# Transfers of the maxima issued ahead of the experts' weights, and twelve unread matmuls between the first scores

## The chip, the cores and the metric

The kernel runs on one core of a Trainium2 chip. A core has five engines that run side by side, each with its own instruction stream: TensorE (PE: matmuls and, as PEld, the loading of their stationary operand), VectorE (DVE), ScalarE (ACT), GpSimd (POOL) and SyncE (SP, which here only issues transfers). They meet through semaphores. Transfers between HBM and the core's memory, and inside that memory, run on 16 DMA engines. The metric is the device time of one execution in microseconds (us). TensorE's clock has two levels here, 2.4 and 1.2 GHz; the profile shows the granted one as PEclk, 1.00 for the higher.

## The reference

```python
def block(x, ctx, lens, Wg, W1, W3, W2, sw1, sw3, sw2):   # x, ctx: (8, 128, 256)
    # attention, 8 heads: the normed x asks, ctx is key and value, and the roles of
    # sequence (128) and width (256) are exchanged: 8 heads of 16 rows, 256 queries, 256 keys
    s = log(lens) / (8 * log(20))                          # one factor per batch entry
    q, k = layernorm(x) in heads of 16 rows, ctx in heads of 16 rows
    x = x + softmax(s * einsum('bhdq,bhdk->bhqk', q, k)) @ v
    # feed-forward: 8 experts of 352 hidden columns, top 1, 128 places each, and a shared one
    xt = layernorm(x).reshape(1024, 256)
    probs = softmax(xt @ Wg); e = argmax(probs); gate = probs[e]
    rows of xt go to their expert's first 128 free places, the rest is dropped
    oe = (silu(xd @ W1[e]) * (xd @ W3[e])) @ W2[e]
    shared = (silu(xt @ sw1) * (xt @ sw3)) @ sw2
    return x + oe[place] * gate * kept + shared
```

The text above is shortened from the reference; all tensors are float32.

## The kernel before

Everything is written out by hand for each engine, with semaphores between them. The first part is attention over 64 units n, one for each of 8 batch entries b and 8 heads. A head has 16 rows of the width-256 dimension, so each unit is a small matmul on 32 of the 128 rows of the array; four heads lie in four blocks of 32 rows.

Attention runs as a pipeline of turns t that every engine walks in the same order. In turn t:

- PE computes the scores of units 2t and 2t+1 (`scores`, L919; in the first LAG = 7 turns four units every second turn, L1030). Each unit is written in two halves u.
- DVE takes the negated row maxima of each unit (`maximum`, L500) into the tile `nm`.
- After the last unit of batch entry b, in turn 4b+4 (`MROW`, L108), PE transposes the maxima (`turn_maxima`, L928), ACT copies them to `mrow` (`maxima_rows`, L739), and SP transfers them from `mrow` into spare rows of the queries `qz` (`load_maxima`, L280 to L285), two transfers for each b. With the maximum as one more row of the contraction, the second scores come out already shifted.
- Seven turns behind, PE computes these shifted and transposed scores (`shifted_scores`, L940), ACT exponentiates them (L746), and PE weighs the values with them (`weigh_values`, L956, from turn 10 on).
- In turns 1 to 8 PE also transposes the context of each batch entry for the values (`turn_values`, L896; turn b+1), and ACT copies it (`values`, L725). Each transpose waits for the copy of the one before.
- `LATE` (L65) says in which turns DVE, ACT and POOL prepare the queries and keys of batch entries 2 and 3, 4 and 5, 6 and 7: statistics from turn 1, 7 and 14, scales and queries one turn later. On ACT, the copy of `values(1)` stands in turn 2 ahead of the statistics of entries 2 and 3 (L717, L719), and DVE's two operations that use them (L465, L468) stand between units 5 and 6 of `maximum`.

`shifted_scores` of the first unit of b waits for that entry's two transfers, `ld_m`. It is issued in turn 7 for b = 0, in turn 11 for b = 1, and so on.

Ahead of the pipeline PE runs 50 idle turns of four small matmuls on a tile of ones (`idle_turn`, L874).

SP issues its transfers strictly in this order: inputs x and context, the shared expert's weights (L319 to L326), then the weights of experts 1 to 4 (`load_expert`, L299 to L307, four transfers each), then a megabyte of zeros that clears the experts' rows in HBM (L330), then for each b the wait for `mrow` and its two transfers, then expert 0. Expert weights are first read after all shared up-projections are done (`expert_high`, L816). The second part of the kernel is the tokens' routing, the shared expert (`shared_up`, L1003 and L1005) and the experts; the change does not touch it.

X is PSUM bank 7, in which PE puts the transposed maxima, outputs and tokens.

Of the kernel before, what the change touches and what calls it, by code (L numbers as in the profile page):

```python
# [42 lines left out]
P = 128  # L43
# [4 lines left out]
E, C, F = 8, 128, 352  # L48
# [10 lines left out]
LAG = 7  # L59
FIRST = 12  # L60
IDLE_TURNS = 50
TURNS = NH // 2
CHUNKS = ((0, 1), (1, 2), (2, 4), (4, 6), (6, B))
EAGER = 2
# [14 lines left out]
NW = 5  # L79
DW = D + 2  # L80
NO_TOKEN = 4 * B * P
LOADS = ((0, 1), (1, 2), (2, 4), (4, E))

END = TURNS + LAG

# [52 lines left out]
def block_kernel(nc, x, ctx_in, lens, wg, w1, w3, w2, sw1, sw3, sw2, consts, out):  # L138
    with ExitStack() as es:
        def sb(name, shape, dt):  # L140
            return es.enter_context(nc.sbuf_tensor(name, shape, dt))

        def sem(name):
            return es.enter_context(nc.semaphore(name))


        xd_dram = nc.dram_tensor("expert_rows", [E * C, DW], F32, kind="Internal").ap()
# [5 lines left out]
        onesb = sb("onesb", [P, P], BF16)  # L153
# [53 lines left out]
        zero = sb("zero", [P, DW], F32)  # L207
# [17 lines left out]
        mx_bank, sc_bank, O, X = bank[0:NS], bank[NS:2 * NS], bank[6], bank[7]  # L225
# [10 lines left out]
        xd_zeroed, xd_sent = sem("xd_zeroed"), sem("xd_sent")  # L236
# [3 lines left out]
        empty_set, numbered = sem("empty_set"), sem("numbered")  # L240
# [32 lines left out]
        @block.sync  # L273
        def _(sp):
            def load_chunk(dst, src, i, done):

                a, z = CHUNKS[i]
                sp.dma_start(dst[:, a:z, :], src[a:z].rearrange("b p d -> p b d")).then_inc(done[i], 16)  # L278

            def load_maxima(b):  # L280

                sp.wait_ge(nm_row, b + 1)
                for half in range(2):
                    sp.dma_start(qz[HD * (1 - half):P:ROWS, b, half, :],
                                 mrow[4 * half:4 * half + 4, b % 2, :]).then_inc(ld_m[b % 2], 16)  # L285

            def load_expert(e):
                n = e % NW
                if e == 0:
                    sp.wait_ge(s_lo, len(SHARED_PIECES))  # L290

                if e == NW:
                    sp.wait_ge(e_up, 1)
                if e == NW + 1:
                    sp.wait_ge(ew_lo, 2)
                if e == NW + 2:
                    sp.wait_ge(ew_lo_2, 1)
                t = wts[n]
                sp.dma_start(t[:, W1:W3].rearrange("p (c f) -> p c f", c=DC),  # L299
                             w1[e].rearrange("(c p) f -> p c f", p=P)).then_inc(ld_w[n], 16)  # L300
                sp.dma_start(t[:, W3:W2].rearrange("p (c f) -> p c f", c=DC),
                             w3[e].rearrange("(c p) f -> p c f", p=P)).then_inc(ld_w[n], 16)
                if e >= NW:
                    sp.wait_ge(e_down, e - NW + 1)
                sp.dma_start(t[:, W2:W2 + 2 * D].rearrange("p (c d) -> p c d", c=2),  # L305
                             w2[e, 0:2 * P].rearrange("(c p) d -> p c d", p=P)).then_inc(ld_w[n], 16)
                sp.dma_start(t[0:FL, W2 + 2 * D:WCOLS], w2[e, 2 * P:F]).then_inc(ld_w[n], 16)  # L307

            load_chunk(xs, x, 0, ld_x)
            sp.dma_start(cst[:], consts).then_inc(ld_cst, 16)  # L310
            sp.dma_start(leni[:], bass.AP(tensor=lens.tensor, offset=lens.offset,
                                          ap=[[0, P], [1, B]])).then_inc(ld_len, 16)
            for i in range(1, len(CHUNKS)):
                load_chunk(xs, x, i, ld_x)
                if i >= EAGER:
                    load_chunk(cs, ctx_in, i, ld_ctx)

            s1 = sraw[:, S1:S3].rearrange("p (c f) -> p c f", c=DC)
            sp.dma_start(s1[:, :, 0:F], sw1.rearrange("(c p) f -> p c f", p=P)).then_inc(ld_shared, 16)  # L319
            sp.dma_start(s1[:, :, F:], wg.rearrange("(c p) f -> p c f", p=P)).then_inc(ld_shared, 16)  # L320
            sp.dma_start(sraw[:, S3:S2].rearrange("p (c f) -> p c f", c=DC),
                         sw3.rearrange("(c p) f -> p c f", p=P)).then_inc(ld_shared, 16)
            sp.dma_start(sraw[:, S2:S2 + 2 * D].rearrange("p (c d) -> p c d", c=2),
                         sw2[0:2 * P].rearrange("(c p) d -> p c d", p=P)).then_inc(ld_shared, 16)
            sp.wait_ge(pad_set, 1)
            sp.dma_start(sraw[0:FL, S2 + 2 * D:], sw2[2 * P:F]).then_inc(ld_shared, 16)  # L326
            for e in range(1, NW):
                load_expert(e)
            sp.wait_ge(empty_set, 2)
            sp.dma_start(xd_dram.rearrange("(n p) d -> p n d", p=P),  # L330
                         zero[:].unsqueeze(1).broadcast_to([P, E, DW])).then_inc(xd_zeroed, 16)
            for b in range(B):
                load_maxima(b)
            load_expert(0)

            sp.wait_ge(xd_sent, 16 * B)
            xd = xd_dram.rearrange("(n p) d -> p n d", p=P)
            for i, (a, z) in enumerate(LOADS):
                sp.dma_start(xe[:, a:z, :], xd[:, a:z, :]).then_inc(ld_xe[i], 16)

            for b in range(B):
                sp.wait_ge(shared_added, b + 1)
                sp.dma_start(out[b], xs[:, b, :]).then_inc(base_stored, 16)
            for e in range(NW, E):
                load_expert(e)
# [103 lines left out]
        def _(dve):  # L449
# [144 lines left out]
            for t in range(END + AFTER):  # L594
                if t < TURNS:
                    maximum(2 * t)
# [102 lines left out]
        def _(act):  # L699
# [82 lines left out]
            for t in range(END + AFTER):  # L782
# [6 lines left out]
                for when, work in ((OUT_COPY, copy_output), (TRSTD, token_rstd)):  # L789
                    if t in when:  # L790
                        work(when.index(t))
                if 0 <= t - LAG < TURNS:
                    exponentials(2 * (t - LAG))
# [75 lines left out]
        def _(pe):  # L869
# [7 lines left out]
            pe.wait_ge(ones_set, 1)  # L877
            for _ in range(IDLE_TURNS):
                for r in range(4):
# [25 lines left out]
            def scores(n, u):  # L905

                b, half, rows = place(n)
                scores_bank = bank[n % (2 * NS) if n < FIRST else n % NS]
                if n % H == 0 and u == 0:
                    if b < EAGER:  # L910
                        pe.wait_ge(k_eager, 2 * (b + 1))
                        pe.wait_ge(q_eager, b + 1)
                        pe.wait_ge(q_made, b + 1)
                    else:
                        pe.wait_ge(k_made, 2 * (b - EAGER + 1))
                        pe.wait_ge(q_made, 2 * (b + 1) - EAGER)
                if n >= 2 * NS and u == 0:
                    pe.wait_ge(maxed, n - 2 * NS + 1 if n < FIRST + NS else n - NS + 1)
                mm = nc.tensor.matmul(scores_bank[:, u * D:(u + 1) * D], qz[rows, b, half, u * P:(u + 1) * P],  # L919
                                      kz[rows, b, half, :], start=True, stop=True)  # L920
                if u == 1:
                    mm.then_inc(scored, 1)
# [102 lines left out]
            for t in range(END + AFTER):  # L1025
                for m in range(NG):
                    for c in range(2):
                        if t == WEIGH[m][c]:
                            weigh_values(m, c)
                if t < LAG and t % 2 == 0:  # L1030
                    heads = range(2 * t, min(2 * t + 4, 2 * LAG))
                    for u in range(2):
                        for n in heads:
                            scores(n, u)
                for part in range(2):
                    for k in range(2):
                        if LAG <= t < TURNS:
                            scores(2 * t + k, part)
                        if 0 <= t - LAG < TURNS:
                            shifted_scores(2 * (t - LAG) + k, part)  # L1040
                for b in range(B):
                    if t == VALUES[b]:
                        turn_values(b)
                for when, work in ((MROW, turn_maxima), (OUT_TURN, turn_output), (OUT_BACK, turn_back),
                                     (TTURN, turn_tokens)):
                    if t in when:
                        work(when.index(t))

                if t in EARLY_UPS:
                    shared_up(EARLY_UPS[t])  # L1050
                if t == EARLY_COUNT:
                    count_tokens(0)
# [136 lines left out]
```

## Time and profile before

| | |
|---|---|
| median of 3 runs | 194.24 us (193.72 to 194.97) |
| the profiled execution | 194.63 us, span 192.7 us |
| mean granted clock | 0.886 |
| PE / PEld busy | 159.4 us (83%) / 112.5 us (58%) |
| DVE, ACT, POOL busy | 104.7, 84.6, 62.7 us |
| DMA queue of SP and ACT | 14240 packets, 14.98 MB |

The span runs from the first to the last instruction. Windows are given in us from its start. The busy time of PE is that of the matmuls in flight, so a PE at 100% may still do little if its matmuls are on few rows or at the lower clock. A wait is put down to the semaphore that came last.

### The profile page before, as it was taken

Reading aid. Unit: us, or ns where it says so; the run is one execution under the profiler, and the core shown is the slowest. Engines: PE = TensorE matmul, PEld = TensorE weight load, DVE = VectorE, ACT = ScalarE, POOL = GpSimd, SP = SyncE. Lnnn points to the kernel's source line nnn. Section 1 sums busy time; section 2 is a strip of 40 time slices with the busy share of each in tenths; the row PEclk is TensorE's granted clock in tenths of the full one; section 3 lists DMA queues with packets and bytes.
Section 4 is the critical chain, followed back from the end, with each engine's and each line's share of the span. In section 5 each row is a group of like instructions: output and inputs, shape, how many; then the busy total and the mean of one; then the engine's idle time right before and its main releaser. Section 6 shows DMA issues by size and latency. Waiting matters only on the chain.

```text
span 192.7 us, 3827 instructions
## 1 busy us (share of the span) xinstructions
PE 159.4 (83%) x1448; PEld 112.5 (58%) x1448; DVE 104.7 (54%) x241; ACT 84.6 (44%) x189; POOL 62.7 (33%) x85
## 2 busy tenths in 40 slices
PE   7679505999998999999999687299893999979960
PEld 7445103555545455555455387298792889779840
DVE  1497202525795978777341433423868238598530
ACT  2632000544747585665757363514751155465000
POOL 5158000092027081432202000044085058535241
PEclk9975555557999999999999999969999799999996
DMA  4999990000000000000070000002025845983001
GB/s 131 343 342 329 322 333 24 0 5 2 2 5 2 3 2 3 2 3 2 0 228 1 2 0 0 3 31 82 0 82 153 292 123 154 306 269 140 29 22 54
DMA packets 15697, 18.44 MB, mean 96 GB/s; under 512 B 1852, under 2 KB 14949, under 8 KB 15680
## 3 DMA queue, kind: packets, MB, share of 16 engines
q1 hardware_dynamic: 14240, 14.98, 25.1%
q0 software_dynamic: 1152, 2.97, 4.6%
q10 hardware_dynamic: 288, 0.26, 0.4%
q8 instruction: 11, 0.18, 0.4%
q14 instruction: 6, 0.05, 0.1%
HBM read 14.12 MB, written 4.21 MB: 95 GB/s over the span
## 4 chain that ended last, share of the span: by engine, by line
PE 62%; SPq 11%; DVE 10%; issue 4%; DMA 4%; POOL 3%; ACT 2%; another core or an unknown queue 2%; DVEq 0%; POOLq 0%; ACTq 0%
PE bank L919 12%; PE bank L940 9%; PE bank L956 8%; PE bank L1003 5%; PE bank L1005 4%; PE bank L1150 4%; DMA qz<-mrow 4%; PE bank L1080 3%; PE bank L1124 3%; PE bank L1125 3%; SPq L278 3%; PE bank L968 2%; SPq L305 2%; DVE xlo L639 2%
## 5 line engine op out<-in xcount | busy, mean ns | idle before, releaser
L500 DVE TENSOR_REDUCE nm<-bank 128x2 f32<-128x512 f32 x64 | 41.1, 685 | 27.4 <-PE bank L919 27.3
L940 PE MATMUL bank<-qz,kz 32*128 32x256 f32 x256 | 46.5, 443 | 9.2 <-DMA qz<-mrow 9.2
L919 PE MATMUL bank<-kz,qz 32*128 32x256 f32 x256 | 43.9, 472 | 2.1 <-POOL qz L358 1.5
L746 ACT ACTIVATE pt<-bank 128x512 f32<-128x512 f32 x64 | 34.6, 589 | 18.0 <-PE bank L940 17.9
L940 PEld LDWEIGHTS bank<-qz,kz 32*128 32x128 f32 x256 | 27.9, 204 | 15.7 <-issue 11.2
L919 PEld LDWEIGHTS bank<-kz,qz 32*128 32x128 f32 x256 | 25.8, 217 | 15.8 <-DVE nm L500 7.4
L956 PE MATMUL bank<-pt,vext 128*32 128x256 f32 x256 | 21.1, 406 | 0.0
L358 POOL TENSOR_SCALAR qz<-xs,rs,mrs 128x256 f32<-128x256 f32 x14 | 7.7, 565 | 39.4 <-DVE mrs L468 39.4
L420 POOL DMA_INDIRECT expert_rows<-rk,idx_s x8 | 8.1, 1012 | 32.6 <-DVE rk L586 30.8
L1150 PE MATMUL bank<-wraw,kz 128*128 128x256 f32 (+1 forms) x48 | 11.8, 386 | 1.8 <-DVE hTlo L646 1.4
L725 ACT COPY vext<-bank 128x256 f32<-128x256 f32 x8 | 3.0, 370 | 23.2 <-PE bank L896 23.2
L443 POOL DMA_INDIRECT out<-vext,rk x8 | 8.2, 1027 | 13.6 <-DVE vext L665 7.2
L436 POOL DMA_INDIRECT vext<-out,rk x8 | 9.2, 1154 | 10.4 <-DMA out<-xs 8.2
L1080 PE MATMUL bank<-shi,hThi 128*128 128x256 f32 x24 | 8.2, 341 | 4.4 <-DVE hTlo L625 4.3
L1150 PEld LDWEIGHTS bank<-wraw,kz 128*128 128x128 f32 (+1 forms) x48 | 8.7, 190 | 3.6 <-DVE kz L660 2.0
L383 POOL TENSOR_TENSOR mrs<-mv,rstd 128x1 f32<-128x1 f32 x6 | 1.1, 189 | 28.3 <-ACT rstd L758 28.3
L956 PEld LDWEIGHTS bank<-pt,vext 128*32 128x32 f32 x256 | 5.2, 110 | 7.2 <-issue 6.2
L591 DVE TENSOR_TENSOR qz<-bank,cs 128x352 f32<-128x352 f32 x8 | 4.1, 522 | 9.3 <-ACT cs L775 7.9
L536 DVE TENSOR_TENSOR xlo<-bank,xhi 128x256 fp32r<-128x256 f32 x8 | 3.4, 425 | 10.5 <-ACT xhi L762 10.5
L639 DVE TENSOR_TENSOR xlo<-wraw,xhi 128x704 fp32r<-128x704 f32 x8 | 8.6, 1112 | 0.0
L1003 PE MATMUL bank<-shi,xhi 128*128 128x360 f32 x16 | 5.9, 367 | 3.3 <-issue 2.8
L1080 PEld LDWEIGHTS bank<-shi,hThi 128*128 128x128 f32 x24 | 5.3, 220 | 5.5 <-DVE hTlo L625 5.3
(140 smaller groups left out, 316.7 us busy)
## 6 DMA issues: line engine op xcount, KB each, us to landing
wraw<-in_w SPq DMA_DIRECT2D x16, 352.0 KB, 7.5
wraw<-in_w SPq DMA_DIRECT2D x8, 256.0 KB, 7.5
expert_rows<-zero SPq DMA_DIRECT2D x1, 1032.0 KB, 10.3
out<-xs SPq DMA_DIRECT2D x8, 128.0 KB, 3.5
xs<-in_x SPq DMA_DIRECT2D x3, 256.0 KB, 6.1
cs<-in_ctx SPq DMA_DIRECT2D x3, 256.0 KB, 6.3
wraw<-in_w SPq DMA_DIRECT2D x8, 96.0 KB, 8.1
wraw<-in_sw SPq DMA_DIRECT2D x2, 352.0 KB, 4.5
```

Source lines behind the costliest of these rows:

```text
L420: nc.gpsimd.indirect_dma_start(xd_dram, bass.IndirectOffsetOnAxis(ap=idx_s[:, b:b + 1], axis=0), x2[:, b, :], None, bounds_check=E * C - 1 ...
L436: nc.gpsimd.indirect_dma_start(res[:, e, :], None, out_rows, number(e), bounds_check=B * P - 1, oob_is_err=False).then_inc(gathered[e], 16)
L443: nc.gpsimd.indirect_dma_start(out_rows, number(e), res[:, e, :], None, bounds_check=B * P - 1, oob_is_err=False).then_inc(out_sent, 16)
L500: nc.vector.tensor_reduce(nm[:, b % 2, :, place], scores_bank[:].rearrange("p (u c) -> p u c", u=2), AX_X, ALU.max, negate=True).then_inc( ...
L639: nc.vector.tensor_tensor(elo[e % 2][:, a:z], wts[e % NW][:, a:z], ehi[e % 2][:, a:z].bitcast(F32), ALU.subtract).then_inc(ew_lo, 1)
L746: nc.scalar.activation(pt[:, g % NPT, n % 4, :], sc_bank[n % NS][:], ACT.Exp).then_inc(exped, 1)
L919: mm = nc.tensor.matmul(scores_bank[:, u * D:(u + 1) * D], qz[rows, b, half, u * P:(u + 1) * P], kz[rows, b, half, :], start=True, stop=True)
L940: mm = nc.tensor.matmul(sc_bank[n % NS][:, c * D:(c + 1) * D], kz[rows, b, half, c * P:(c + 1) * P], qz[rows, b, half, :], start=True, sto ...
L956: mm = nc.tensor.matmul(O[32 * j:32 * j + 32, g * D:(g + 1) * D], vext[:, b, c, h, :], pt[:, m % NPT, i, c * D:(c + 1) * D], start=(c == 0 ...
L1003: nc.tensor.matmul(u1, xpart[:, b, c, :], weights(part, S1, F + WG, c, F + WG), start=a, stop=z)
L1080: mm = nc.tensor.matmul(y_bank[b % 2][:, 0:D], hpart[:, b % 2, c * P:(c + 1) * P], weights(part, S2, D, c, D), start=(k == 0), stop=(k == ...
L1150: mm = nc.tensor.matmul(y_bank[(e + 1) % 2][:, 0:D], hTe[0:rows, e % 2, c * P:(c + 1) * P], wts[e % NW][0:rows, W2 + c * D:W2 + (c + 1) * ...
```

## The change

Two edits. SP's list is rewoven: the wait and the two transfers of the maxima of b now stand ahead of the weights of expert b+1, for b = 0 to 3, and the zeros stand behind the maxima of b = 4. PE runs six matmuls of 512 columns over the tile of ones into bank X behind the scores of turn 0 and six behind those of turn 2; nothing reads their result.

```diff
+UNREAD = {0: 6, 2: 6}
...
-            for e in range(1, NW):
-                load_expert(e)
-            sp.wait_ge(empty_set, 2)
-            sp.dma_start(xd_dram.rearrange("(n p) d -> p n d", p=P),
-                         zero[:].unsqueeze(1).broadcast_to([P, E, DW])).then_inc(xd_zeroed, 16)
             for b in range(B):
                 load_maxima(b)
+                if b + 1 < NW:
+                    load_expert(b + 1)
+                if b + 1 == NW:
+                    sp.wait_ge(empty_set, 2)
+                    sp.dma_start(xd_dram.rearrange("(n p) d -> p n d", p=P),
+                                 zero[:].unsqueeze(1).broadcast_to([P, E, DW])).then_inc(xd_zeroed, 16)
             load_expert(0)
...
                     for u in range(2):
                         for n in heads:
                             scores(n, u)
+                    for _ in range(UNREAD.get(t, 0)):
+                        nc.tensor.matmul(X[:].rearrange("p (n c) -> p n c", c=P), onesb[:],
+                                         onesb[:].unsqueeze(1).broadcast_to([P, 4, P]), start=True, stop=True)
```

On SP, this is the end of the initial loads in the kernel before: the weights of the fourth expert (`wraw<-in_w`), the zeros (`expert_rows<-zero`), all sixteen transfers of maxima (`qz<-mrow`), and the first transfer of expert 0.

```order
L299 DMA wraw<-in_w 128x2x352
L301 DMA wraw<-in_w 128x2x352
L305 DMA wraw<-in_w 128x2x256
L307 DMA wraw<-in_w 96x256
L330 DMA expert_rows<-zero 128x8x258
L284 DMA qz<-mrow 4x256 x16
L299 DMA wraw<-in_w 128x2x352
```

In the changed kernel, SP goes on like this behind the last transfer of the shared weights (its line numbers are one higher).

```order
L327 DMA wraw<-in_sw 96x256
L285 DMA qz<-mrow 4x256 x2
L300 DMA wraw<-in_w 128x2x352
L302 DMA wraw<-in_w 128x2x352
L306 DMA wraw<-in_w 128x2x256
L308 DMA wraw<-in_w 96x256
L285 DMA qz<-mrow 4x256 x2
L300 DMA wraw<-in_w 128x2x352
```

The first two transfers of maxima have moved from behind sixteen transfers of weights and the zeros to the place ahead of them.

On PE, turns 0 to 7 before: scores (`bank<-kz,qz`), transposes for the values (`bank<-cst,cs`), the transpose of the first maxima (`bank<-cst,nm`), and the first shifted scores (`bank<-qz,kz`).

```order
L919 MATMUL bank<-kz,qz 128x256 x8
L896 MATMUL bank<-cst,cs 128x128 x2
L919 MATMUL bank<-kz,qz 128x256 x8
L896 MATMUL bank<-cst,cs 128x128 x4
L919 MATMUL bank<-kz,qz 128x256 x8
L896 MATMUL bank<-cst,cs 128x128 x2
L928 MATMUL bank<-cst,nm 8x128 x2
L896 MATMUL bank<-cst,cs 128x128 x2
L919 MATMUL bank<-kz,qz 128x256 x4
L896 MATMUL bank<-cst,cs 128x128 x2
L919 MATMUL bank<-kz,qz 128x256
L940 MATMUL bank<-qz,kz 128x256
```

The same stretch of the changed kernel, up to the transpose of the maxima (line numbers two higher).

```order
L921 MATMUL bank<-kz,qz 128x256 x8
L1038 MATMUL bank<-onesb 128x512 x6
L898 MATMUL bank<-cst,cs 128x128 x2
L921 MATMUL bank<-kz,qz 128x256 x8
L1038 MATMUL bank<-onesb 128x512 x6
L898 MATMUL bank<-cst,cs 128x128 x4
L921 MATMUL bank<-kz,qz 128x256 x8
L898 MATMUL bank<-cst,cs 128x128 x2
L930 MATMUL bank<-cst,nm 8x128 x2
```

The two groups of six stand between the scores and the transposes for the values; nothing else on PE changed its place.

## Rows read from the trace of the kernel before

**Rows 1.** The page's strip of transfers: the span in 40 slices of 4.8 us.

```profile
GB/s 131 343 342 329 322 333 24 0 5 2 2 5 2 3 2 3 2 3 2 0 228 1 2 0 0 3 31 82 0 82 153 292 123 154 306 269 140 29 22 54
```

**Rows 2.** Waits from 7 to 32 us: who for whom, us, times, longest.

```profile
PE bank L940 <- DMA qz<-mrow: 9.2, 1, 9.2
```

**Rows 3.** Chain of work that ended last, 17 to 36 us: start, us, what.

```profile
23.89 7.01 DMA qz<-mrow
...
31.04 0.76 PE bank L940
```

**Rows 4.** Instructions in order of time: start, us, engine (q: its sequencer), line.

```profile
17.26 0.36 ACT L739 COPY mrow<-bank 8x256 f32<-8x256 f32 x1
...
21.40 3.00 SPq L284 DMA_DIRECT2D qz<-mrow  x2
```

**Rows 5.** The same view, 7 to 21 us, PE, DVE and ACT.

```profile
7.51 1.15 PE L919 MATMUL bank<-kz,qz 32*128 32x256 f32 x16 [1.52 <-POOL qz L358]
...
9.53 2.48 DVE L500 TENSOR_REDUCE nm<-bank 128x2 f32<-128x512 f32 x4
...
11.92 0.57 PE L896 MATMUL bank<-cst,cs 128*128 128x128 f32 x2
...
12.53 0.37 ACT L725 COPY vext<-bank 128x256 f32<-128x256 f32 x1 [2.53 <-PE bank L896]
...
13.63 2.54 PE L919 MATMUL bank<-kz,qz 32*128 32x256 f32 x16
...
14.23 1.28 DVE L500 TENSOR_REDUCE nm<-bank 128x2 f32<-128x512 f32 x2
...
16.59 0.63 PE L928 MATMUL bank<-cst,nm 128*8 128x128 f32 x2
...
20.57 1.22 PE L919 MATMUL bank<-kz,qz 32*128 32x256 f32 x2
```

**Rows 6.** Windows: length, busy PE PEld DVE ACT POOL, clock, DMA share, GB/s.

```profile
12.00:13.00 1.00, 0.49 (x2) 0.12 (x2) 1.00 (x6) 0.46 (x2) 0.09 (x1) 0.54 1.11 320
```

**Rows 7.** Windows by stage, same columns.

```profile
15.60:20.60 5.00, 4.87 (x22) 2.33 (x17) 3.04 (x5) 1.11 (x3) 3.12 (x6) 0.50 1.08 319
20.60:31.00 10.40, 1.19 (x3) 0.46 (x2) 0.74 (x2) 0.37 (x1) 0.00 (x0) 0.50 0.90 275
31.00:46.55 15.55, 15.52 (x100) 8.35 (x100) 6.46 (x14) 5.62 (x13) 5.71 (x10) 0.51 0.01 2
46.55:50.42 3.87, 3.87 (x54) 2.12 (x51) 2.58 (x4) 2.88 (x6) 0.00 (x0) 1.00 0.01 2
68.63:77.47 8.84, 8.84 (x108) 4.82 (x107) 7.01 (x14) 5.57 (x14) 4.23 (x7) 1.00 0.01 3
97.80:101.20 3.40, 3.40 (x34) 1.84 (x34) 1.56 (x5) 2.02 (x4) 0.00 (x0) 1.00 0.88 295
101.20:104.60 3.40, 3.40 (x34) 1.72 (x32) 0.15 (x1) 3.12 (x8) 1.41 (x2) 1.00 0.02 2
```

**Rows 8.** Instructions in order of time, where turn 12 begins.

```profile
46.55 0.64 PE L956 MATMUL bank<-pt,vext 128*32 128x256 f32 x8
```

**Rows 9.** The maxima of b = 2: the copy, then a window of half a microsecond.

```profile
49.30 0.34 ACT L739 COPY mrow<-bank 8x256 f32<-8x256 f32 x1
...
51.30:51.80 0.50, 0.50 (x14) 0.48 (x11) 0.50 (x1) 0.33 (x1) 0.00 (x0) 1.00 0.03 8
```

**Rows 10.** Instructions in order of time: idle turns, and 118 to 119 us.

```profile
1.01 4.97 PE L874 MATMUL bank<-onesb 32*128 32x128 bf16 x200 [1.01 <-POOL onesb L352]
...
118.84 0.33 PE L1003 MATMUL bank<-shi,xlo 128*128 128x360 f32 x1
119.00 0.32 PE L1005 MATMUL bank<-shi,xlo 128*128 128x352 f32 x1
```

**Rows 11.** Instructions in order of time, PE alone, 121 to 125 us.

```profile
121.03 0.44 PE L983 MATMUL bank<-cst,rk 128*128 128x128 f32 x2 [1.70 <-DVE rk L531]
...
124.38 0.40 PE L1003 MATMUL bank<-shi,xhi 128*128 128x360 f32 x1 [2.83 <-issue]
```

## The prediction

> **What bounds the kernel now.** I read the stages first, then the waits, then the chain. The page's strip of transfers shows the queue full from 5 to 29 us [rows 1]. Over the same time the table by stage shows PE doing little: from 20.6 to 31.0 us it is busy for 1.19 of 10.40 us [rows 7]. The waits name one event: `shifted_scores` of turn 7 waits 9.2 us for the transfer of the first maxima [rows 2]. The chain says the same: 7.01 us of `qz<-mrow`, then L940 at 31.04 [rows 3]. The maxima themselves were ready long before: ACT wrote them by 17.62, SP issued them only at 21.40 [rows 4], because sixteen transfers of weights and the zeros stand ahead, and the 8 KB then had to go through a queue that those had filled. Nothing else ends that wait.
>
> The second thing is the clock. It is at the lower level, 1.2 GHz, from 12.5 us [rows 6] until just before 46.55, where PE's window reads 0.51 and the next one 1.00 [rows 7]. Before it fell, PE ran only scores 4 to 7, sixteen instructions on 32 rows each like the group at 7.51 [rows 5], and a transpose, and waited for DVE between them. In the lower state turns 7 to 11 took 15.5 us (31.04 to 46.55) [rows 3, 8], 3.1 us each; turns 12 and 13 then took 3.87 us, 1.94 each, and a block of four turns with every kind of work in it 8.84, 2.21 each [rows 7]. PE sets the pace in both. In all windows shown behind turn 12, up to 104.6 us, PE is busy throughout [rows 7], so whatever turn 12 gains should arrive at the end.
>
> **The change part by part.** I follow PE to two moments: the start of turn 7 (31.04 before) and of turn 12 (46.55 before).
>
> *The unread matmuls.* Their price has no row. The nearest from below is the shared up-projection, two instructions of 360 columns 0.16 us apart [rows 10]: 512 columns would be 0.23, six 1.4 us. From above, the idle turns: four blocks of 128 columns side by side per 0.0994 us (4.97/50) [rows 10] make 512 columns 0.40, six 2.4 us. At the higher clock I take 1.4, since the up-projection also uses all 128 rows and stands at that level.
>
> The first six start at 8.66 and end about 10.1. DVE takes its first maximum only at 9.53 and is busy with four until 12.01 [rows 5], and scores 4 to 7 need only be there by then, so these six are hidden; if DVE were not late they would cost their 1.4 us. The second six start where `turn_values(1)` stood, 11.92, and are not hidden: that transpose, and ACT's copy behind it at 12.53 [rows 5], come 1.4 us later. Behind this copy ACT holds the statistics of entries 2 and 3; DVE's scales wait for them and stand ahead of units 6 and 7 of the maxima (14.23 to 15.51) [rows 5]. Before, the scales had about no slack, so units 6 and 7 end about 1.2 us later, at 16.7. On PE, scores 8 to 11 took 2.54 us from 13.63 at the lower clock; at the higher the like-sized group took 1.15 [rows 5]. They start at about 15.0 and end at 16.1, before DVE's 16.7. So the transpose of the maxima comes at 16.8 instead of 16.59, and ACT's copy ends at about 17.7 instead of 17.62. The two effects nearly cancel.
>
> *The transfers of the maxima.* SP now issues at 17.7. What it has issued by then is x, the context, the constants and the shared weights, 3.35 MB by their shapes, which at 343 GB/s [rows 1] is 9.8 us: the queue is empty at about 13. For an empty queue, the maxima of b = 2: copied by 49.64, last bytes moved between 51.3 and 51.8 [rows 9], so 1.7 to 2.2 us. The bound from above is what happened before, 9.5 us from issue to landing (21.40 to 30.9), which the full queue made. I take 2.2: landing at 19.9. PE is there by about 18.5 (before 20.57 [rows 5], with 5 us of work from 15.6 at the lower clock [rows 7]), so it waits some 1.4 us and turn 7 starts at 19.9. Gain there: 31.04 - 19.9 = 11.1 us.
>
> *Turns 7 to 11.* If the clock is held, they go at 1.94 to 2.21 us a turn [rows 7], 9.7 to 11.1 us. DVE alone bounds them from below: two maxima 1.28 us [rows 5] in every turn and one us of statistics, at least 7.4. Turns 7 to 9 have no weighing yet, 7 and 8 have a transpose for the values more. I take 2.0, 10.0 us: turn 12 at 29.9 instead of 46.55. Gain there: 16.6 us, of which 5.5 come from the clock in these turns.
>
> *The weights and zeros.* They now run during attention, 5.3 MB or 16 us of the queue at 343 GB/s, each of the four experts between two groups of maxima. From 97.8 to 101.2 us such weights ran at 295 GB/s and PE began 34 instructions, as many as in the 3.4 us behind it at 2 GB/s [rows 7]; so I price their company at nothing. They land by about turn 20 and are first read after 110 us; were that cover gone, an expert's 1056 KB would cost 3.6 us at 295 GB/s. SP has nothing else queued behind its new waits until expert 0, whose place is the same.
>
> *Sum.* 194.63 (the profiled execution) - 16.6 = 178.0. Its time is 0.4 above the median shown, so 177.6 for the median.
>
> **Whether the clock stays up** is what I know least. Between the second six (end 13.3) and turn 7 (19.9) PE has scores 8 to 13 and a row of transposes, and waits at the end. One row for such a stretch: around 121 us PE had two transposes and little else between 119.2 and 124.4, with waits of 1.70 and 2.83 us [rows 11], and behind it the clock was at the lower level for a while. My stretch is denser, and the one that preceded the fall at 12.5 had the waits without the unread matmuls. I lean to the clock being held. The Trainium skill ("TensorE: Matmul & The Clock Gate", Part 4: PE-mode transpose) says that work in transpose mode does not count for the gate as matmuls do. If so, PE's transposes between the two groups and turn 7 do not help, and the clock falls there, as in the first rival below: by that rule 183.1 where the sum says 177.6. The row at 121 us agrees with it as far as it goes, but waits stand beside the transposes there, so it doesn't separate them.
>
> **The rivals.**
> - *The clock falls while PE transposes and waits for the maxima* (about 16 to 20 us). Turn 7 starts at 19.9, but turns 7 to 11 take their 15.5 us as before: turn 12 at 35.4, gain 11.1, 183.1 for the median. For it: those turns at the lower clock did not bring it back until their end, although PE was busy for 15.52 of 15.55 us [rows 7]. A fall only after two or three of these turns gives about 180.
> - *The unread matmuls don't hold the clock at 12.5 us.* The second six then cost up to 2.4 us, DVE and PE are late by 1.5 to 2, turn 7 starts at about 22.5: gain 8.5, 185.7. Against it: full rows for 2.8 us in a stretch where PE was on quarter rows.
> - *The wait stays, behind other weights.* Maxima of b = 1 to 4 now follow an expert each. If a group lands only behind the expert ahead of it, with 3.6 us of transfer and up to 9.5 us from issue, against three turns of slack (5.8 us), four waits of 3.7 us make 15 us. With the clock lost too (gain 11.1) the kernel would be slower, at 198; with the clock held, 192.4. It decides only if an expert's weights are still in the queue when the next copy is done; but SP issues them 8.8 us (four turns) earlier, against 3.6 us of transfer. Little speaks for it.
> - *The first wait was not the queue*: the transfers take 9.5 us even on an empty queue. Then turn 7 starts at 27.2, and a PE that waits so long again keeps no clock: gain 3.8, 190.4. The copy of b = 2 [rows 9] speaks against it.
>
> **How the numbers follow.** Clock held 0.52; falls before or in the first turns of turn 7 and later 0.30; not held at 12.5 us 0.12; wait stays behind other weights 0.03, of which 0.02 end slower; first wait not the queue 0.03. The case of 177.6 has its own range of 175.5 (turns 7 to 11 near DVE's bound) to 179.5 (2.21 a turn, and stretches of low clock that shift in the last part). For 8 in 10 the range must take in the falling clock, 180 to 184, so 175.5 to 185.0. About 1% is what a measurement of this kernel can tell from no change. All cases of a shorter first wait are faster by more: 0.96 faster, 0.02 same, 0.02 slower.
>
> **What would show it.** Right: no wait of L942 longer than 2 us; `qz<-mrow` issued at 17 to 18 us and nothing of `wraw<-in_w` ahead of it; clock 1.00 from 9 to 50 us; turn 12 (first L958 of the third group) at about 30 us; transfers low after 13 us, and the experts' weights in bursts of 3 to 4 us until about 60. Wrong: clock 0.50 at 22 us (first rival) or at 13 (second); a wait of L942 on `qz<-mrow` in turns 11, 15 or 19 (third). If turn 12 comes at 30 and the end is not 16 us earlier, the gain was given back behind attention, which I hold to be unchanged.

## The result and the profile after

| | before | changed |
|---|---|---|
| median of 4 runs | 193.98 us (192.56 to 194.97) | 178.21 us (176.30 to 181.00) |
| ratio of the faster executions | | 0.911 (95% interval 0.901 to 0.921) |
| profiled execution / its span | 194.63 / 192.7 | 181.00 / 178.1 |
| first scores (L919, L921) | 7.51 | 8.47 |
| transpose of the first maxima (L928, L930) | 16.59 | 18.05 |
| turn 7: first shifted scores (L940, L942) | 31.04 | 21.32 |
| turn 12: its weighing (L956, L958) | 46.55 | 31.25 |
| last group of weighing starts | 107.41 | 91.98 |

By the medians the change is faster by 15.8 us, 8.1%, and 0.6 us from the 177.6 forecast. The ratio of 0.911 counts only two of the changed kernel's four executions, those of 176.30 and 176.86 us, which ran at a mean granted clock of 0.974 and 0.971; the other two took 179.55 us (0.950) and, the profiled one, 181.00 us (0.955). The same kernel run again (e0 below) gave 0.921. The times in the table are from the profiled executions; rows of the changed kernel have line numbers two higher on PE, DVE and ACT, and one higher on SP.

Where the 9.2 us wait was, the chain of the changed kernel (start, length, what) goes straight through:

```profile
8.47 2.02 PE bank L921 x16
10.49 2.16 PE bank L1038 x6
12.66 0.22 PE bank L898 x2
12.88 1.07 PE bank L921 x16
13.95 1.40 PE bank L1038 x6
15.35 0.23 PE bank L898 x2
...
15.61 0.37 ACT vext L727
15.98 0.20 ACT lnv L719
...
16.21 0.21 ACT rstd L721
...
16.44 0.17 DVE rs L467
...
16.80 1.21 DVE nm L502 x2
...
18.05 0.40 PE bank L930 x2
...
18.48 0.37 ACT mrow L741
...
18.86 0.66 SPq L285
...
19.57 1.61 DMA qz<-mrow
...
21.32 0.45 PE bank L942
```

Both groups of unread matmuls (L1038) stand on it, then ACT's copy and the statistics behind it, DVE's scales and its next two maxima, and the maxima's own path. The transfer takes 1.61 us on the chain instead of 7.01 [rows 3]. The same steps in order of time show PE's wait for it, 0.32 us where there were 9.2 [rows 2], and DVE's for ACT:

```profile
16.44 0.16 DVE L467 SCALAR_TENSOR_TENSOR rs<-rstd,lnown 128x4 f32<-128x4 f32 x1 [1.18 <-ACT rstd L721]
...
18.86 1.21 SPq L285 DMA_DIRECT2D qz<-mrow  x2
...
21.32 0.45 PE L942 MATMUL bank<-qz,kz 32*128 32x256 f32 x1 [0.32 <-DMA qz<-mrow]
```

By stage, with the columns of [rows 7] (length, busy PE PEld DVE ACT POOL, clock, DMA share, GB/s):

```profile
9.00:11.00 2.00, 2.00 (x18) 1.05 (x11) 1.34 (x5) 0.97 (x2) 1.52 (x3) 0.50 1.09 359
11.00:13.00 2.00, 2.00 (x12) 0.88 (x13) 2.00 (x5) 0.09 (x1) 1.33 (x3) 0.75 0.98 317
13.00:21.00 8.00, 7.27 (x60) 3.91 (x57) 6.61 (x16) 2.91 (x9) 4.10 (x8) 1.00 0.04 12
21.32:31.25 9.93, 9.15 (x100) 5.33 (x100) 6.78 (x16) 5.63 (x14) 4.64 (x9) 1.00 0.49 151
31.25:92.00 60.75, 59.43 (x671) 32.01 (x670) 40.07 (x86) 38.84 (x89) 18.84 (x28) 1.00 0.26 85
...
105.00:116.00 11.00, 7.57 (x34) 7.50 (x35) 3.82 (x16) 3.40 (x8) 3.23 (x4) 0.69 0.07 26
```

Turns 7 to 11 take 9.93 us with a hundred PE instructions at clock 1.00, where the same hundred took 15.55 at 0.51 [rows 7]. In windows of 0.2 us the clock fell at 8.6 us and was back at 12.0 (hence 0.75 in the row from 11 to 13); after that it was low only for a while in the last part. The fall came before the first unread matmul, which starts at 10.4. The experts' weights run beside the turns (151 GB/s) instead of ahead of them.

### The profile page after: what moved, and what is told of

The parts are those of the page before. It is cut to its first block, busy times and chain, and to the rows that moved or that the text cites. A ratio compares the mean times of both kernels' runs of the same rounds, so it can differ in the third digit from the quotient of the medians.

```text
span 178.1 us, 3851 instructions
## 1 busy us (share of the span) xinstructions
PE 152.3 (85%) x1460; PEld 109.1 (61%) x1460; DVE 105.7 (59%) x241; ACT 84.8 (48%) x189; POOL 63.8 (36%) x85
## 4 chain that ended last, share of the span: by engine, by line
PE 66%; DVE 12%; DMA 7%; issue 4%; ACT 4%; POOL 3%; SPq 1%; POOLq 0%; ACTq 0%; DVEq 0%
PE bank L921 12%; PE bank L958 8%; PE bank L942 8%; PE bank L1005 5%; PE bank L1007 5%; PE bank L1155 5%; PE bank L1085 4%; PE bank L1129 3%; PE bank L1130 3%; DMA wraw<-in_w 3%; DVE xlo L641 3%; DMA leni<-in_lens 3%; PE bank L970 2%; DVE nm L502 2%; PE bank L1038 2%
## 5 line engine op out<-in xcount | busy, mean ns | idle before, releaser
L942 PE MATMUL bank<-qz,kz 32*128 32x256 f32 x256 | 41.2, 403 | 1.1 <-ACT pt L748 0.8
L921 PE MATMUL bank<-kz,qz 32*128 32x256 f32 x256 | 36.3, 420 | 2.5 <-POOL qz L360 2.5
L921 PEld LDWEIGHTS bank<-kz,qz 32*128 32x128 f32 x256 | 21.7, 190 | 13.3 <-issue 8.9
L942 PEld LDWEIGHTS bank<-qz,kz 32*128 32x128 f32 x256 | 24.9, 184 | 6.7 <-ACT pt L748 4.2
L958 PE MATMUL bank<-pt,vext 128*32 128x256 f32 x256 | 20.2, 391 | 0.0
L445 POOL DMA_INDIRECT out<-vext,rk x8 | 9.0, 1123 | 12.8 <-DMA vext<-out,rk 6.1
L641 DVE TENSOR_TENSOR xlo<-wraw,xhi 128x704 fp32r<-128x704 f32 x8 | 10.0, 1283 | 0.0
L958 PEld LDWEIGHTS bank<-pt,vext 128*32 128x32 f32 x256 | 5.2, 108 | 6.6 <-issue 6.3
L777 ACT ACTIVATE cs<-bank 128x352 f32<-128x352 f32 x8 | 3.6, 464 | 11.1 <-PE bank L1007 11.0
```

Of the source, the lines that this page charges most:

```text
L445: nc.gpsimd.indirect_dma_start(out_rows, number(e), res[:, e, :], None, bounds_check=B * P - 1, oob_is_err=False).then_inc(out_sent, 16)
L641: nc.vector.tensor_tensor(elo[e % 2][:, a:z], wts[e % NW][:, a:z], ehi[e % 2][:, a:z].bitcast(F32), ALU.subtract).then_inc(ew_lo, 1)
L942: mm = nc.tensor.matmul(sc_bank[n % NS][:, c * D:(c + 1) * D], kz[rows, b, half, c * P:(c + 1) * P], qz[rows, b, half, :], start=True, sto ...
L958: mm = nc.tensor.matmul(O[32 * j:32 * j + 32, g * D:(g + 1) * D], vext[:, b, c, h, :], pt[:, m % NPT, i, c * D:(c + 1) * D], start=(c == 0 ...
```

## Experiments

Every kernel was run with a profile and then, unless said otherwise, three more times, beside the kernel before on the same chip. The kernel before gave medians of 194.50 us beside e0 to e3, 193.31 beside e5 to e8 and 193.82 beside e9 to e12. Leaving one execution of the kernel before of 449 us aside, it stayed between 192.4 and 195.2 throughout.

| run | median, range (us) | turn 7 | first scores to L930 | mean clock of the executions |
|---|---|---|---|---|
| changed, first profile | 178.21 (176.3 to 181.0) | 21.32 | 9.58 | 0.955 0.950 0.974 0.971 |
| e0 changed again | 178.52 (177.7 to 179.6) | 20.83 | 9.59 | 0.950 0.954 0.961 0.956 |
| e1 maxima only | 182.70 (178.8 to 184.5) | 21.19 | 9.35 | 0.912 0.912 0.909 0.949 |
| e2 unread only | 194.13 (191.9 to 196.1) | 30.80 | 9.59 | 0.895 to 0.914 |
| e3 transposes | 177.00 (175.9 to 177.6) | 18.35 | 7.33 | 0.968 0.967 0.966 0.968 |
| e5 second six only | 178.04 (176.9 to 183.9) | 21.23 | 10.14 | 0.906 0.967 0.965 0.960 0.957 |
| e6 twenty-four | 181.17 (178.2 to 182.7) | 21.33 | 10.53 | 0.974 0.926 0.937 0.952 |
| e7 75 idle turns | 177.80 (177.3 to 178.5) | 20.70 | 7.91 | 0.967 0.968 0.964 0.965 |
| e8 75, no unread | 178.24 (176.1 to 184.2) | 21.25 | 8.11 | 0.949 0.974 0.913 0.961 |
| e9 behind the values | 178.45 (176.9 to 185.3) | 18.93 | 7.33 | 0.961 0.946 0.964 0.916 |
| e10 transposes, behind | 178.41 (176.2 to 181.9) | 18.54 | 7.78 | 0.970 0.966 0.934 0.936 |
| e11 weights last | 179.68 (177.0 to 180.2) | 20.18 | 9.59 | 0.956 0.957 0.954 0.964 |
| e12 transposes again | 177.81 (175.5 to 178.3) | 19.95 | 8.38 | 0.955 0.965 0.962 0.967 |

Turn 7 and the distance are of the profiled execution, the first of each list of clocks. Of the other executions only the time and the mean clock are known: that one "lost the clock" is read from a mean of 0.90 to 0.94 together with a long time, and where in the kernel it was lost is not shown. The first scores themselves start between 7.3 and 8.5 us with 50 idle turns, whatever the kernel (9.5 and 9.9 with 75); what moves them is told in the last section.

### The two parts apart (e0, e1, e2)

e0 is the changed kernel. 

> The changed kernel as it is, beside the runs below on the same chip. Theory (wait gone and clock held): turn 7 at 20 to 21.5 us, clock 1.00 from there to past 100 us, 176 to 180 us. Rival (part of the executions lose the clock in the first turns): the times of single executions fall in two groups, some near 177 and some at 180 or above.

178.52 us, 0.921 (0.914 to 0.929) of before. Turn 7 at 20.83; the clock was low from 8.2 to 11.6 us, then at 1.00 to past 100. No execution reached 180 us, as the rival had it. There are two at 177.7 and 177.8 and two at 179.2 and 179.6, but their mean clocks (0.961 and 0.950, 0.956 and 0.954) do not set these pairs apart.

e1 leaves the unread matmuls out.

```diff
-UNREAD = {0: 6, 2: 6}
+UNREAD = {}
```

> Only the transfers of the maxima are moved; no unread matmuls. If the two parts are worth what the prediction says (11.1 us the wait, 5.5 us the clock), this is about 183 us: turn 7 (first L942) at 20 to 21 us, the clock at 0.50 there, and turns 7 to 11 take about 15.5 us. Rival, the clock is held by the missing wait alone: about 178 us, and the unread matmuls are worth nothing.

182.70 us. The profiled execution is the forecast's first rival in pure form (same columns):

```profile
9.00:13.00 4.00, 3.10 (x22) 1.61 (x20) 3.55 (x10) 1.59 (x5) 2.85 (x5) 1.00 1.00 314
13.00:21.00 8.00, 7.34 (x34) 4.34 (x34) 5.92 (x14) 2.35 (x7) 4.30 (x8) 0.54 0.08 17
21.00:34.00 13.00, 13.00 (x80) 7.20 (x78) 6.03 (x14) 4.91 (x12) 4.83 (x10) 0.50 0.38 125
34.00:50.00 16.00, 14.92 (x188) 8.12 (x188) 12.75 (x27) 10.75 (x24) 4.88 (x8) 1.00 0.33 104
```

The clock fell at 13.6 us and was back at 34.0, and PE walked turns 7 to 10 at 0.50 with its matmuls in flight for 13.00 of 13.00 us. Turn 7 came at 21.19, as with the unread matmuls, turn 12 at 36.07 instead of 30.77. But one of the four executions had a mean clock of 0.949 and took 178.79 us, as the changed kernel does. So without unread work the clock is lost often, not always. The parts are then 11.3 to 11.8 us for the transfers (to 193.98 and 194.50), and 4.2 us by the medians for the unread matmuls. These 4.2 us are a matter of how often the clock is kept: three of four executions lost it here, none of eight of the changed kernel; an execution that keeps it is no slower without them.

e2 keeps the unread matmuls and has SP's order as before.

> Only the twelve unread matmuls; SP's order as before. Theory: the wait for the first maxima stays until about 31 us, PE stands idle for 10 us, the clock falls in it whatever was run before, turns 7 to 11 take 15.5 us: 194 us, within 1% of before. Rival, the unread matmuls help by themselves: below 191.5 us with the clock at 1.00 before 40 us.

194.13 us in ten executions, ratio 0.998 (0.993 to 1.003). The stages:

```profile
12.60:22.60 10.00, 7.52 (x62) 4.11 (x60) 7.21 (x16) 3.00 (x9) 4.32 (x9) 0.99 1.09 321
22.80:30.80 8.00, 0.00 (x0) 0.03 (x1) 0.00 (x0) 0.00 (x0) 0.00 (x0) 0.50 0.94 282
30.80:46.50 15.70, 15.70 (x104) 8.37 (x108) 6.45 (x14) 5.62 (x13) 5.71 (x10) 0.51 0.01 3
```

and its wait:

```profile
PE bank L941 <- DMA qz<-mrow: 10.0, 1, 10.0
```

Here too the clock was low from 8.7 to 12.1 us. Then, with the unread matmuls on PE, it stayed at 1.00 where the kernel before ran at 0.50; PE stood still for the maxima from 21 us, the clock fell at 22.3, and turns 7 to 11 took what they had before. Alone, this part is worth nothing: its 4.2 us exist only once the wait is gone.

### What kind of unread work (e3, e12)

```diff
-nc.tensor.matmul(X[:].rearrange("p (n c) -> p n c", c=P), onesb[:],
-                 onesb[:].unsqueeze(1).broadcast_to([P, 4, P]), start=True, stop=True)
+nc.tensor.transpose(X[:, 0:P], cs[:, 0, 0:P], ident)
```

> As the changed kernel, but the twelve unread matmuls of 512 columns are twelve unread fp32 transposes of 128 columns, which the profile of before shows at the same 0.21 us each. If a transpose keeps the clock as a matmul does: 176 to 180 us, clock 1.00 in turns 7 to 11. If transposes do not count for the clock as matmuls do: turn 7 at the same time, but the clock at 0.50 in turns 7 to 11, about 183 us, as with no unread work at all.

177.00 us, 0.910 (0.904 to 0.917), the four executions within 1% of each other. The clock stayed at 1.00 from 7 us to past 100:

```profile
7.00:13.00 6.00, 4.77 (x48) 3.48 (x48) 5.33 (x17) 2.72 (x8) 3.40 (x6) 1.00 1.00 315
13.00:18.00 5.00, 4.72 (x36) 2.79 (x36) 4.96 (x11) 2.17 (x7) 4.07 (x8) 1.00 0.08 25
18.35:28.29 9.94, 9.16 (x100) 5.33 (x100) 6.79 (x16) 5.63 (x14) 4.64 (x9) 1.00 0.51 155
28.30:89.00 60.70, 59.38 (x668) 31.98 (x666) 40.09 (x86) 38.83 (x89) 18.76 (x28) 1.00 0.26 84
```

So the transposes, as this kernel issues them, did the unread matmuls' work. They are also shorter than I had expected of them:

```profile
8.83 0.88 PE L1038 MATMUL bank<-cst,cs 128*128 128x128 f32 x6
9.54 0.38 PE L898 MATMUL bank<-cst,cs 128*128 128x128 f32 x2
9.86 1.65 PE L921 MATMUL bank<-kz,qz 32*128 32x256 f32 x16
11.43 0.87 PE L1038 MATMUL bank<-cst,cs 128*128 128x128 f32 x6
```

Six end in 0.88 us instead of the matmuls' 1.47. Turn 7 started at 18.35, 2.5 us before e0: 0.2 by earlier first scores, the rest by a distance of 7.33 instead of 9.59, most of it because the clock never fell (with the matmuls and no fall, e7 below, it is 7.91).

e12 is the same kernel on another chip. 

> The kernel with unread transposes at the places of the twelve matmuls once more, beside the two above on the same chip. Theory: 176 to 178 us and, as the first time, all executions within 1%; the changed kernel's executions spread over 1 to 2.5%. Rival, the first time was luck of the clock: executions above 180 us among them.

177.81 us, 0.909 (0.902 to 0.917). Here the clock did fall in the profiled execution, from 9.5 to 12.9 us, and turn 7 came at 19.95. None of the eight executions of e3 and e12 took more than 178.3 us or had a mean clock below 0.955; the eight of the changed kernel lie between 176.3 and 181.0. The medians of the eights are 177.4 and 178.5; the intervals of the ratios overlap, so "0.6% better" is not shown. No run found a version that is clearly better than the change.

### Which group, and how much (e5, e6)

e5 keeps the second group alone.

```diff
-UNREAD = {0: 6, 2: 6}
+UNREAD = {2: 6}
```

> As the changed kernel, with the six unread matmuls behind turn 2 only. The first six cost 2.2 us where they ran at the lower clock. Theory: the clock in turns 7 to 11 hangs on the stretch from 12 to 20 us, which the second six fill, so it is held without the first, and turn 7 starts 1 to 2 us earlier: 176 to 178 us. Rival, the first six are needed to bring the clock back after it fell at about 9 us: clock 0.50 in turns 7 to 11 of the profile, 181 to 184 us.

178.04 us. The profiled execution took 183.87 and is the only one of five that lost the clock in the turns:

```profile
8.00:14.80 6.80, 6.80 (x39) 3.98 (x40) 5.31 (x14) 1.68 (x5) 2.85 (x5) 0.53 0.77 242
15.00:21.00 6.00, 5.20 (x40) 2.77 (x38) 4.60 (x10) 2.62 (x8) 4.18 (x8) 1.00 0.00 1
21.70:35.00 13.30, 13.30 (x88) 6.66 (x83) 6.08 (x14) 5.40 (x13) 5.71 (x10) 0.50 0.46 157
```

The clock was low from 7.6 us, came back at 14.4 while the second six ran (13.27 to 15.1), and fell again at 21.2. The other four took 176.9 to 180.0, as the changed kernel. With one in five against none in eight, the worth of the first six stays open.

e6 has twelve in each place.

```diff
-UNREAD = {0: 6, 2: 6}
+UNREAD = {0: 12, 2: 12}
```

> Twenty-four unread matmuls, twelve behind turn 0 and twelve behind turn 2. It prices them. If only the second group lies on the path, as predicted (1.4 us for six), 1.4 us more than the changed kernel: 180 us. If both groups do, 2.8 us or more: 181 to 182 us. If neither does, no change: 178.5 us.

181.17 us, in the range of the case in which both groups lie on the path. But the median doesn't price the matmuls: the two longest executions, 182.4 and 182.7 us, ran at a mean clock of 0.926 and 0.937, and the profiled one, at 0.974, took 178.22 us. The profile does. It has no fall of the clock before 100 us, and DVE's wait for ACT in the place named above:

```profile
16.46 0.16 DVE L467 SCALAR_TENSOR_TENSOR rs<-rstd,lnown 128x4 f32<-128x4 f32 x1 [2.48 <-ACT rstd L721]
```

From the first scores to the transpose of the maxima it takes 10.53 us, against 7.91 in e7, the kernel with twelve whose clock did not fall: 2.6 for twelve more matmuls, 0.22 each. So beyond twelve, every unread matmul in either place stands on the path in full.

### More work ahead of the scores (e7, e8)

```diff
-IDLE_TURNS = 50
+IDLE_TURNS = 75
```

> The changed kernel with 75 idle turns ahead of the scores instead of 50, so that PE is not idle from 6 to 8 us. In the changed kernel the clock fell at about 9 us for 3.4 us, with the first six unread matmuls in it. Theory: that fall comes from PE's idle time between the idle turns and the first scores; with it filled the clock is 1.00 from 6 us on, the first six take 1.4 instead of 2.2 us, turn 7 starts 1 to 2 us earlier: 176 to 177 us, and single executions lie closer together. Rival, the fall has another cause: same as the changed kernel, 178.5 us.

177.80 us, 0.918 (0.910 to 0.926). The clock did not fall before 100 us, the first six took 1.47, and the four executions lie within 0.7%, as the theory had it. But turn 7 came hardly earlier (20.70 against 20.83 in e0), since the first scores came later:

```profile
8.43 1.27 PE L876 MATMUL bank<-onesb 32*128 32x128 bf16 x77 [2.64 <-issue]
9.51 0.47 PE L921 MATMUL bank<-kz,qz 32*128 32x256 f32 x4
```

In the middle of the idle turns PE stood for 2.64 us, waiting for nothing that the profile shows. So the gap was moved, not filled, and the theory, that the fall comes from it, was not tested by this run. Other profiles speak against it: in e9 PE stood for 3.11 us ahead of the first scores and the clock did not fall, in e11 for 1.86 and it did. The queries were ready at 8.14 us here, and PE came to the scores only at 9.51.

e8 takes the unread matmuls out of this kernel.

> 75 idle turns, the maxima first, and no unread matmuls. Theory: it is PE's thin work from 9 to 20 us that loses the clock; more work before it does not help: clock 0.50 in turns 7 to 11, 182 to 184 us, like the kernel with the maxima only. Rival, the idle turns do the unread matmuls' work at no price on the path: 175 to 177 us.

178.24 us: neither theory. In the profile the clock fell at 8.5 us and came back at 12.0 with no unread work behind the scores (77 of the idle matmuls ran from 8.17 to 10.15), and stayed at 1.00 through turns 7 to 11; of the other three executions one, at 0.913 and 184.2 us, lost it. So it behaves as e1 does, one in four here against three in four there; that the idle turns made this difference is not shown by four executions each.

### The place on PE (e9, e10)

In both, the unread work of turns 0 and 2 stands behind `turn_values(0)` and `turn_values(1)` instead of ahead of them: e9 with the matmuls, e10 with the transposes of e3.

```diff
+for _ in range(UNREAD.get(t, 0)):     # now behind turn_values(b) of turn t; UNREAD = {1: 6, 2: 6}
```

> The changed kernel with the second six unread matmuls behind the transpose of values(1) instead of ahead of it (the first six behind that of values(0), in the same gap). In the changed kernel the step that made them cost was: transpose, ACT's copy, the statistics of entries 2 and 3 behind it on ACT, DVE's scales, and only then maxima 6 and 7. Theory: with the transpose ahead of them they fill the time in which PE waits for ACT's copy anyway; DVE's scales come right behind its maxima 4 and 5, and turn 7 starts 1 us earlier: about 177 us against 178.5. Rival, the place does not matter: 178.5 us.

In the profiled execution the step is as the theory says. ACT's copy comes at once, and DVE's scales follow its own maxima without a wait:

```profile
12.64 0.37 ACT L727 COPY vext<-bank 128x256 f32<-128x256 f32 x1 [2.37 <-PE bank L898]
...
12.90 1.26 DVE L502 TENSOR_REDUCE nm<-bank 128x2 f32<-128x512 f32 x2
13.02 0.29 ACT L719 ACTIVATE lnv<-mv,epst 128x2 f32<-128x2 f32 x1
...
14.07 0.15 DVE L467 SCALAR_TENSOR_TENSOR rs<-rstd,lnown 128x4 f32<-128x4 f32 x1
```

The distance to L930 is 7.33 us, as in e3, instead of 7.91 with the clock up in both (e7), and 9.59 in e0. So at the higher clock the place is worth 0.6 us. Yet the median is 178.45, no better: one execution lost the clock and took 185.3, one took 179.6.

> Twelve unread transposes in place of the twelve matmuls (0.145 us each in the run with transposes, against 0.23), behind the transposes of the values as in the run before. Theory: the shortest unread work at the place where it costs least, so the earliest turn 7, at 18 to 18.5 us, and 175.5 to 176.5 us. Rival, with so little work so late the clock falls in some executions: 176 to 182 us with a wide spread.

178.41 us, 0.909 (0.903 to 0.915) by the two executions of 176.2 and 176.5 us. Turn 7 at 18.54 was as expected, but the other two ran at 0.934 and 0.936 and took 180 to 182. That is what the rival said of the times; where these two lost the clock was not profiled.

### The company of the weights (e11)

SP's list has the weights of experts 1 to 4 and the zeros behind the maxima of b = 7.

> The changed kernel with the weights of experts 1 to 4 and the zeros behind all maxima, so that no large transfer runs during attention until about 80 us. It prices the company of these transfers and their place between the maxima. Theory (they cost nothing): turns 12 to 36 take the same time to 0.3 us, turn 7 starts at the same time, and the end is the same unless the weights are now late for the experts: 178 to 179 us. Rival, the transfers slow PE, ACT or DVE or delay maxima: turns 12 to 36 are shorter by 1 us or more.

179.68 us, 0.918 (0.910 to 0.926). From the weighing of turn 12 to the last group of weighing, in e11 and then in e0:

```profile
30.12 0.64 PE L957 MATMUL bank<-pt,vext 128*32 128x256 f32 x8
...
90.84 1.07 PE L957 MATMUL bank<-pt,vext 128*32 128x256 f32 x16
```

```profile
30.77 0.64 PE L958 MATMUL bank<-pt,vext 128*32 128x256 f32 x8
...
91.49 1.07 PE L958 MATMUL bank<-pt,vext 128*32 128x256 f32 x16
```

60.72 us in both, and from the first scores to turn 7 12.84 and 12.85. The weights between the maxima cost attention nothing that these two profiles show, neither by their traffic nor by their place in the queue. The median is 0.7 us above the forecast's range. In the profile the part behind the last weighing takes 85.8 us against 84.5 in e0; the weights now come there (260 GB/s from 90.8 to 103 us), but that they cause the 1.3 us was not tested.

## Why the prediction was right, and where it was not

**The wait for the maxima** was the queue, as forecast. From the transpose of the maxima to turn 7 I had 3.1 us (16.8 to 19.9); it took 3.27, and 3.25 to 3.26 in e0, e3 and e9. With a queue emptied of weights the transfer takes 1.61 us on the chain. The rival in which it takes 9.5 us on an empty queue is gone. Turn 7 came 9.7 us earlier, not 11.1: 1.0 of the difference is the later start of the scores (8.47 against 7.51), which follows the landing of `in_lens` and not the change (last section), 0.3 the distance to the transpose of the maxima (the price of the unread matmuls, below), 0.2 the path behind it.

**Turns 7 to 11** I had at 10.0 us at the higher clock; they took 9.93, and 9.94 in e0 and e3. With it the gain at turn 12 is 15.3 us instead of 16.6, and it reached the last weighing unchanged: from turn 12 to there 60.73 us against 60.86 before. Behind it 86.1 us against 85.3; the clock was low there for longer (0.69 over eleven us, against 0.84 over the like eleven before, from 120.4 us). That is why the profiled execution gained 14.6 us in its span.

**The sum.** It was made for the profiled execution: 194.63 - 16.6 = 178.0. That execution took 181.00, so the sum missed by 3.0: 1.3 at turn 12, 0.7 from there to the end of the span, and 1.0 outside the span (1.9 before, 2.9 after), for which the prediction had no term. That the median comes to 0.6 us of the forecast is in part luck: it is the middle of two executions near 176.6 and two near 180.3, and none of the four took 177 to 179. The four of e0 lie closer to it, with a median of 178.52.

**The price of the unread matmuls.** 0.23 us each at the higher clock: six took 1.40 on the chain, as forecast; 2.16 at the lower. The failed step is "these six are hidden", said of the first group. They were costed against DVE, which indeed waited only 0.17 us for scores 4 to 7. But `turn_values(1)` stands behind both groups, and through ACT's copy it sets DVE's scales; I had counted that chain for the second group alone. The chain above carries both, and e6 prices both. A second slip went the other way: "about no slack" for DVE's scales. In the kernel before, ACT's statistics ended at 13.44 and the scales started at 13.96, 0.5 us of slack; and the scores and transposes around the unread work, at the higher clock, get there sooner. So where the clock never falls the twelve together lengthen the distance by about 0.6 us (7.91 in e7, 7.33 in e9 and e3), not by the 1.2 that I had for the second six alone. In the profiled execution the low clock from 8.6 to 12.0 us ate that: distance 9.58 us, beside the 9.3 that I had in effect. That these two numbers are close is luck.

**The clock.** "Clock 1.00 from 9 to 50 us" was wrong in the profile: it was low from 8.6 to 12.0 us. The prediction also read the fall before at 12.5 us; its own row (0.54 from 12 to 13) puts it at 12.1. In the changed kernel the clock came back at 12.0 while the first six ran (10.43 to 12.66); in e5, which has scores there instead, it stayed low with PE in flight for 6.80 of 6.80 us and came back at 14.4, while its only six ran. From this pair it looks as if dense unread work brings the clock back early, but that is argued: e8 was back at 12.0 without any. That unread work keeps the level in turns 7 to 11 rests on none of eight executions that lost it with the matmuls, none of eight with the transposes of e3 and e12, and three of four without. The level in turns 7 to 11, which mattered for the sum, was as forecast.

**The first rival** (clock lost in the turns, 183.1 us) is what e1 is in three of four executions (182.3 to 184.5), and what single executions of e5, e8 and e9 are (183.9 to 185.3; those of e8 and e9 by time and mean clock alone). None of the eight of the changed kernel has a mean clock below 0.950. The page's rule that spoke for it (the Trainium skill, "TensorE: Matmul & The Clock Gate", Part 4: PE-mode transpose) is not borne out by the transposes of this kernel: in e3 they were all the unread work there was, and the clock was 1.00 from 7 us on. Whether they run in the mode that the page means, no row shows. The measurement decides.

**The second rival**, clock not held at 12.5 us: in the profile it fell earlier, at 8.6, for 3.4 us, and was back when the second six ran, so they cost 1.40 and not 2.4. **The third**, a wait behind other weights: of all 256 matmuls of L942 only the first waits for `qz<-mrow`, for 0.3 us, and e11 gives the same 60.72 us.

What stays open is why an execution keeps the clock and the next, with the same kernel, does not. e1, e5, e6, e8, e9 and e10 show that it happens, with no unread work and with up to twenty-four matmuls of it; four executions of each are too few to rank them.

## What to carry to other kernels

A small transfer that a compute engine waits for belongs ahead of bulk loads that are needed later, if the issuing engine can afford the wait for its data; look for it as one long wait on a transfer whose source was written long before. Ahead of a stretch in which TensorE sets the pace, thin work and a standstill can cost twice, once in time and once in the clock of what follows (turns 7 to 11: 15.5 us at 0.51, 9.9 at 1.00); unread work there paid only after the standstill itself was gone. Count what stands behind such filler on its own engine through every chain, and judge it by several executions, since the clock of one proves little.

## What was not expected of the hardware

- Six unread fp32 transposes of 128 columns took 0.88 us, although a pair of the same kind is shown at 0.38. The time of a group holds the tail of its last matmul: by these two groups four more cost 0.50, 0.13 each. In the same way six more matmuls of 512 columns cost 1.29 (2.76 for twelve in e6, 1.47 for six), 0.22 each.
- PE stopped for 2.64 us (e7) and 1.92 us (e8) inside 300 independent matmuls on one tile, both times behind the 223rd, with no wait that the profile shows. What it waits for there was not tested. In e7 the queries were ready at 8.14 us and in e8 at 7.00, and the scores came at 9.51 and 9.88, so more filler ahead of the scores delayed them.
- The start of the first scores moved by 1.1 us (7.34 to 8.47) between executions of kernels with the same instructions up to there. With 50 idle turns it follows one small transfer, `in_lens`: DVE converts the lengths as soon as they land, and the scales and the first queries wait for that. The conversion (L481, `lenf<-leni`, waiting for the transfer of `leni`) started at 5.30 us in the kernel before, 5.13 in e11, 5.77 in e0 and 6.26 in the changed kernel, and the first scores came 2.21 us behind it each time. Making that transfer land sooner was not tried.
